# A decoder layer on one core: GpSimd takes the low half of the attention output and the first two normalisations, and the bias of v goes through the output weight once

## The reference, cut to what matters

```python
def attn(x, Wqkv, bqkv, Wo, bo):              # 16 heads of 32
    kqv = (x @ Wqkv + bqkv).reshape(b, s, 3, 16, 32)
    q, k, v = kqv[:, :, 0], kqv[:, :, 1], kqv[:, :, 2]
    scores = einsum('bsnh,btnh->bnst', k, q) / sqrt(32)
    scores = triu(scores) + -10000.0 * tril(ones, k=-1)
    attn = softmax(scores, axis=2)            # over s
    out = einsum('bnkq,bknh->bqnh', attn, v).reshape(b, s, 512)
    return out @ Wo + bo
def step(carry, kv_t):                        # wkv: a scan over t, per channel
    p, q, o = carry; kt, vt = kv_t
    no = maximum(o, u + kt); A = exp(o - no); E = exp(u + kt - no)
    y = (A * p + E * vt) / (A * q + E)
    no2 = maximum(w + o, kt); A2 = exp(w + o - no2); E2 = exp(kt - no2)
    return (A2 * p + E2 * vt, A2 * q + E2, no2), y
x = layernorm(x + attn(x))                    # x: 4 x 512 x 512, float32
x = layernorm(x + wkv(w, u, x, ctx))
x = layernorm(x + down(silu(gate(x)) * up(x)))  # inner width 2048
```

## Time and profile before

| | |
|---|---|
| median of 3 runs | 837.01 us (836.72 to 838.01) |
| the profiled execution | 835.81 us, its span 834.0 us |
| busy in the span | PE 743.1, DVE 558.8, ACT 408.3, POOL 271.2 us |
| granted TensorE clock, mean | 0.959 of full speed |

### The profile page before, as it was taken

How to read it: one execution, slowest core, us unless ns; L and a number is a source line. 1 busy time by engine, 2 the same in 40 slices (tenths; PEclk the granted TensorE clock), 3 DMA queues, 4 the chain that set the end, 5 groups by cost and what they waited for, 6 DMA issues and landing times.

```text
span 834.0 us, 11936 instructions
## 1 busy us (share of the span) xinstructions
PE 743.1 (89%) x4256; PEld 404.1 (48%) x4256; DVE 558.8 (67%) x1217; ACT 408.3 (49%) x1000; POOL 271.2 (33%) x284
## 2 busy tenths in 40 slices
PE   5988699978889978999677598889999999999997
PEld 2555456644456545565443254434454444444443
DVE  4455545778998879998898488874774544344434
ACT  5568767777567776686846213302332034104310
POOL 2001233328341155500346515541622133103320
PEclk9999799998999989999979899999999999999999
DMA  7246494232034122141620610001000100010001
GB/s 248 62 138 217 139 215 127 89 114 65 13 89 139 44 72 77 33 117 56 133 44 1 101 51 1 1 13 39 2 1 13 38 1 1 14 38 1 1 13 38
DMA packets 44331, 54.17 MB, mean 65 GB/s; under 512 B 4720, under 2 KB 33648, under 8 KB 44272
## 3 DMA queue, kind: packets, MB, share of 16 engines
q1 hardware_dynamic: 41008, 47.11, 18.0%
q0 software_dynamic: 3264, 6.29, 4.4%
HBM read 47.10 MB, written 12.58 MB: 72 GB/s over the span
## 4 chain that ended last, share of the span: by engine, by line
PE 59%; DVE 18%; issue 6%; POOL 6%; ACT 5%; DMA 3%; SPq 3%; POOLq 0%; DVEq 0%; ACTq 0%
PE psb L717 20%; PE psb L607 7%; PE psb L730 6%; PE psb L728 6%; PE psb L697 5%; PE psb L654 4%; DVE ek L1034 4%; DVE ee L946 3%; PE psb L621 2%; SPq L1270 2%; PE psb L643 2%; DMA xt<-in_xT 2%; PE psb L665 2%; PE psb L704 1%; PE psb L633 1%
## 5 line engine op out<-in xcount | busy, mean ns | idle before, releaser
L946 DVE CUSTOM_DVE_ANT_0 ee<-psb,mask,clip 128x512 f32<-128x512 f32 (+3 forms) x256 | 131.0, 530 | 54.7 <-PE psb L643 54.1
L810 ACT ACTIVATE ee<-ee,nm 128x512 f32<-128x512 f32 (+3 forms) x256 | 142.8, 559 | 32.4 <-DVE nm L946 32.1
L654 PE MATMUL psb<-ident,ee 128*128 128x128 f32 x640 | 108.5, 288 | 25.9 <-ACT ee L821 25.7
L821 ACT ACTIVATE ee<-psb 128x512 f32<-128x512 f32 (+1 forms) x192 | 100.0, 521 | 56.4 <-PE psb L654 56.1
L1212 POOL TENSOR_TENSOR hl<-hf,hh 128x512 f16<-128x512 f32 x64 | 77.5, 1211 | 134.9 <-ACT hh L884 134.9
L884 ACT ACTIVATE hh<-hf 128x512 bf16<-128x512 f32 x64 | 40.4, 632 | 144.1 <-DVE hf L1059 144.1
L717 PE MATMUL psb<-x2h,wg 128*128 128x512 f16 x256 | 99.5, 389 | 6.6 <-DVE th L1049 5.9
L654 PEld LDWEIGHTS psb<-ident,ee 128*128 128x128 f32 x640 | 76.3, 147 | 54.2 <-ACT ee L821 34.5
L717 PE MATMUL psb<-x2l,wg 128*128 128x512 f16 x256 | 99.7, 390 | 0.0
L730 PE MATMUL psb<-wd,hl 128*128 128x512 f16 x256 | 97.0, 379 | 2.3 <-POOL hl L1212 2.3
L717 PE MATMUL psb<-x2h,wu 128*128 128x512 f16 x256 | 97.5, 381 | 0.0
(11 more groups left out here) (106 smaller groups left out, 1236.3 us busy)
## 6 DMA issues: line engine op xcount, KB each, us to landing
qs<-parts SPq DMA_DIRECT2D x64, 128.0 KB, 2.7
ks<-parts SPq DMA_DIRECT2D x64, 128.0 KB, 2.9
parts<-qhl SPq DMA_DIRECT2D x16, 256.0 KB, 2.1
parts<-khl SPq DMA_DIRECT2D x16, 256.0 KB, 2.1
x<-in_x SPq DMA_DIRECT2D x4, 1024.0 KB, 7.8
ct<-in_ctxT SPq DMA_DIRECT2D x4, 1024.0 KB, 6.2
out<-x SPq DMA_DIRECT2D x16, 256.0 KB, 2.0
xt<-in_xT SPq DMA_DIRECT2D x14, 256.0 KB, 4.0
```

What stands on the lines that cost most here:

```text
L654: mm = e.transpose(PSB[:, bk, o:o + P], E[H % 3][:, EOFF[i] + j * P:EOFF[i] + (j + 1) * P], IDENT[:])
L810: e.activation(dst, dst, ACT.Exp, bias=NM[:, n % 4, col:col + 1], scale=-1.0, accum_out=DEN[:, n % 4, col:col + 1]).then_inc(sem("exp"), 1)
L821: e.activation(ET[h][:, base:base + width], PSB[:, bank["turn", H, item], 0:width], ACT.Copy).then_inc(sem("et"), 1)
L946: e.tensor_tensor_reduce(E[H % 3][:, EOFF[i]:EOFF[i] + w], PSB[:, bank["score", H, i], 0:w], MASK[:, S - w:S], -SC, CLIP[:, i:i + 1], ALU. ...
```

## The change

Four things are edited. `ol` becomes a plain subtraction on GpSimd, two slots after `normed` rather than four. `norm` of kinds 0 and 1 is done on GpSimd, directly behind `rstd`; kind 2 stays on VectorE. `oh` no longer adds the bias. Instead the bias is multiplied with the output weight once: four f32 matmuls (`bvo`) whose stationary operand is one column of `BV` repeated 128 times and whose moving operand is the f32 output weight in `CT`, and one add on VectorE (`bo`) into `BO`. `add_bo` waits for that add, and the load that overwrites `CT` waits for `bvo` as well.

```diff
     "pv": lambda n: ("t2", n),
+    "bvo": lambda: ("bo",),
...
         return lambda: (late(1, lambda: add("t3", n)), late(1 + hold, lambda: add("oh", n)),
-                        late(4 + hold, lambda: add("ol", n)))
+                        late(2 + hold, lambda: add("ol", n)))
...
                     if what == "split_wo":
-                        add("load_ct", 0)
+                        tt.unit("bvo")
+                        add("bvo")
+                        late(1, lambda: (add("bo"), add("load_ct", 0)))
...
+        def bvo():
+            emptied(("bvo",))
+            pe.wait_ge(sem("wo_in"), 16)
+            pe.wait_ge(*by_consts())
+            for k in range(T):
+                mm = e.matmul(PSB[:, bank["bvo",], :], BV[:, k:k + 1].broadcast_to([P, P]), CT[:, k, :], start=(k == 0),
+                              stop=(k == T - 1))
+            mm.then_inc(sem("bvo"), 1)
...
-            e.activation(oh[:, g, :], EB[:], ACT.Identity, bias=BV[:, g:g + 1]).then_inc(sem("oh"), 1)
+            e.activation(oh[:, g, :], EB[:], ACT.Copy).then_inc(sem("oh"), 1)
...
-        def o_low(n):
-            g = n % T
-            dve.wait_ge(*by("oh", n))
-            e.scalar_tensor_tensor(out=ol[:, g, :], in0=EB[:], scalar=BV[:, g:g + 1], in1=oh[:, g, :], op0=ALU.add,
-                                   op1=ALU.subtract).then_inc(sem("ol"), 1)
...
+            elif name == "bo":
+                dve.wait_ge(*by("bvo"))
+                dve.wait_ge(*by_consts2())
+                e.tensor_tensor(BO[:], PSB[:, bank["bvo",], :], BO[:], ALU.add).then_inc(sem("bo"), 1)
...
+        def norm(kind, b, t0, t1):
+            z = 4 * kind + b
+            pool.wait_ge(*by("rstd", kind, b, t0, t1))
+            for t in range(t0, t1):
+                e.tensor_scalar(X[b][:, t, :], X[b][:, t, :], MV[:, z, t, 0:1], RS[:, z, t:t + 1], ALU.subtract,
+                                ALU.mult).then_inc(sem(f"norm{kind}"), 1)
+
+        def o_low(n):
+            pool.wait_ge(*by("oh", n))
+            e.tensor_tensor(ol[:, n % T, :], EB[:], oh[:, n % T, :], ALU.subtract).then_inc(sem("ol"), 1)
...
-                pool.wait_ge(*by_consts2())
+                pool.wait_ge(*by("bo"))
...
                     sp.wait_ge(sem("wol"), T)
+                    sp.wait_ge(*by("bvo"))
```

More of the change, by code:

```diff
@@ L752, in _ @@
                 wo_part(*a)
+            elif name == "bvo":
+                bvo()
             elif name == "x1t":
@@ L1003, in rstd, with norm @@
             e.tensor_scalar(VE[:, z, t0:t1], MV[:, z, t0:t1, 1], EPS, None, ALU.add).then_inc(sem("ve"), 1)
-        def norm(kind, b, t0, t1):
-            z = 4 * kind + b
-            dve.wait_ge(*by("rstd", kind, b, t0, t1))
+        def norm(b, t0, t1):
+            dve.wait_ge(*by("rstd", 2, b, t0, t1))
             for t in range(t0, t1):
-                e.tensor_scalar(X[b][:, t, :], X[b][:, t, :], MV[:, z, t, 0:1], RS[:, z, t:t + 1], ALU.subtract,
-                                ALU.mult).then_inc(sem(f"norm{kind}"), 1)
+                e.tensor_scalar(X[b][:, t, :], X[b][:, t, :], MV[:, 8 + b, t, 0:1], RS[:, 8 + b, t:t + 1], ALU.subtract,
+                                ALU.mult).then_inc(sem("norm2"), 1)
         def scan_q(b, c):
@@ L1096, in _ @@
                 t3(*a)
-            elif name == "ol":
-                o_low(*a)
+            elif name == "bo":
+                dve.wait_ge(*by("bvo"))
+                dve.wait_ge(*by_consts2())
+                e.tensor_tensor(BO[:], PSB[:, bank["bvo",], :], BO[:], ALU.add).then_inc(sem("bo"), 1)
             elif name == "split_wo":
@@ L1116, in _ @@
                 rstd(*a)
-            elif name == "norm":
-                norm(*a)
+            elif name == "norm" and a[0] == 2:
+                norm(*a[1:])
             elif name == "scan_q":
@@ L1233, in _ @@
                 rstd(*a)
+            elif name == "norm" and a[0] != 2:
+                norm(*a)
+            elif name == "ol":
+                o_low(*a)
             elif name == "ek":
```

## The result

The change made the kernel slower: 860.66 us, median of four runs (857.04 to 861.06), against 836.87 us of the kernel before beside them (835.25 to 838.01). The ratio is 1.0276, with a 95% interval of 1.0244 to 1.0309: 23.8 us more, where 6 less were forecast. The profiled execution, the fastest of the four, took 857.04 us, its span 855.2 us.

A forecast was written before the change was run, and what follows sets the result against it. VectorE was taken to bound the attention's scan stretches, TensorE other parts, including everything from about 570 us. Terms -2.2 - 2.5 - 2.5 + 0.45 + 0.8 = -5.95 took 837.0 to 831.0 us; range 822 to 838.5.

The forecast's parts named there:

- The price of the norm: Norm instruction on GpSimd: 0.65 us each, four in 2.6 us against 1.92 on VectorE; upper bound 1.275 us.
- the rival at 840: Norms on GpSimd at the two-input price make the kernel slower: +2.9 us, 839.9 us; chance 0.12.
- The slower rival: Four norms on GpSimd take 5.1 us, making `d`, `x1t` and `hl` late: +2.9, 839.9 us; chance 0.12.
- Term A: Start of the feed-forward part: VectorE, freed of two norm holds, does its units earlier; -2.2 us, bounds 0 and -5.8.
- Term B: VectorE's full scan stretches without `ol`: -0.6 us for each of three scans, -0.7 before the third; -2.5 us.
- Term C: Five attention norms off VectorE: kind 1 -0.9 us each, kind 0 -0.2 to -0.3 each; -2.5 us together.
- Term D: What gets later: output product waiting for the last `ol`, +0.45 us; `ol` ahead of the last `xl`, +0.8.
- The bias through the weight: Four f32 products near 82 us cost nothing, as TensorE soon idles there; without that cover 4.2 us, once.

The follow-up runs named there:

- the run with the norms alone: The kernel before with only the norms of kinds 0 and 1 moved to GpSimd, as subtraction and multiplication; 855.67 us, 1.0219.
- the best version: The kernel before with only the norms of kinds 0 and 1 on GpSimd, written as addition then multiplication; 833.58 us, 0.9958.
- the run with the norms back: The changed kernel with all norms again on VectorE, `ol` on GpSimd and the bias through the output weight kept; 843.14 us, 1.0067.

## Why the prediction was wrong, point by point

- **The price of the norm is the step that failed.** I wrote that it "has one tensor input and two operations, as L1163 has", and so took 0.65 us, with 1.275 as the upper bound. It measured 2.11. The count of inputs and operations doesn't set the price; which operations they are does. L1163 multiplies and adds (0.65), the norm subtracts and multiplies. A bound "by the nearest two-input row" is no bound for another operation either: that was the worse fault, since it cut off the rival at 840.
- **The slower rival had the mechanism.** It named `d` behind the norm, three places, `x1t` and the second norm between two `hl`. With 8.3 us for four its own arithmetic gives 3 × 4.8 for `d` and 4.3 for `x1t`, 18.7 us; measured in the run with the norms alone: 4.8 at each of the three, 4.0, and 3.1 behind them, less 1.1 for each of the two norms of kind 1, where it had 0.9. Its point of decision, about 1.0 to 1.07 us an instruction, agrees with both sides measured in the kernel before: 0.82 us is faster, 2.1 slower. Nothing between was run.
- **Term A** (-2.2): by the price it became a loss of 4.0 us at the first norm. At 0.82 us the way from the first to the second inverse deviation took 5.6 us instead of 6.6, so 1.0 came back, and the 2.17 us wait of the earlier trace rows shrank to 1.41 and wasn't gone.
- **Term B** (-2.5) was wrong in itself for the order that the change has. Where -0.6 stood for each of three scans, the change measured -0.85, +0.8 and +0.7 (8.84 - 9.69, 8.51 - 7.73, 8.40 - 7.74). These three distances are the same within 0.02 us in the traces of all nine kernels with `ol` on GpSimd ahead of the denominator, and likewise in the five with it on VectorE. I put the denominator 1.3 us later, at 223.2, with the reciprocal free at 223.1. But beside VectorE's scans `ol` took 1.81 us, the product behind it 1.72 and the denominator 2.06, so that the reciprocal waited 0.85 us. The Trainium skill, "SBUF — State Buffer", section "Who interferes with whom", says that GpSimd and a two-input VectorE instruction exclude each other; by that rule I had worked out 0 for this term. The trace agrees with it as far as it goes (`ol` 1.16 us alone, 1.81 beside a scan), and the loss beyond 0 is the place in the queue: behind the denominator the same three distances are 2.5 us shorter than before (8.04, 7.29, 7.30). The whole kernel is no faster than before even so (1.0005); what takes the 2.5 us back isn't shown, and the bias through the weight is in that kernel too. The -0.7 for the `ol` ahead of the third scan wasn't measured apart.
- **Term C** (-2.5): the two norms of kind 1 gave 1.1 us each where -0.9 stood, at 0.82 us (milestones 265.85 to 282.47 before, 267.28 to 282.78 in the best version) and at 2.1 us as well (267.57 to 283.07 in the change). The three of kind 0 gave 0.4 each in the best version, where 0.2 to 0.3 stood, and cost 4.8 each at 2.1 us. That term was right, at its price. Terms A and C together stood at -4.7; the best version has -3.8.
- **Term D**: the wait of the output product for the last `ol` went from 3.8 to 4.2 us, +0.4, as forecast 0.45. The `ol` ahead of the last `xl` can't be read apart.
- **The bias through the weight** cost 0 to 3.4 us, 1.8 in the middle, where 0 stood; it is not settled whether it costs anything. The products themselves cost what I said or less (3.60 us for the four, at 80.15). If there is a cost, the traces point to the later load of `xt` in batch 3, of which the prediction says nothing.
- **Not in the sum at all**: the clock. After new waits TensorE can stand at its lower level for some microseconds, as behind the 4.40 us, and the mean granted clock of the change is 0.942 against 0.959. How much of the 24 us this is wasn't measured apart.

What stays open: how the 6 us of the run with the norms back divide. The place of `ol` ahead of the three denominators is 3.1 us against the place behind them, but only 0.6 against `ol` on VectorE. 1.7 are the stretch at the lower clock, with a cause that isn't shown. The rest is within what the bias may cost. I haven't run the cheap norm for kind 1 alone, or an `ol` in yet another place.

## What to carry to other kernels

A price taken from a row holds for its operations, not for its shape: before work is moved to another engine, put the exact instruction (operations, order, scalars) into a kernel and read its duration. On an in-order queue, ask of a moved block not who needs its result but what stands behind it; a block longer than the idle time ahead of the next urgent instruction only changes who waits when it is moved along. If a price is out of line, look for another way to write the same arithmetic: `(x - m) * r` as `(x + (-m)) * r` turned 2.1 us into 0.82. With the place of `ol` mended as well it turned a loss of 24 us into a small gain (0.9978), and alone in the kernel before it gave the best version (0.9958).

## What the runs showed of the hardware that I had not expected

- GpSimd's `tensor_scalar` on 128x512 f32, each as the median of its set: 0.62 us for add-multiply, multiply-add and multiply-multiply with constants (0.69 with one scalar from memory, 0.77 with two, 0.82 as the mean over a whole kernel); 1.48 to 1.49 for a single add, subtract or multiply; 1.91 to 1.93 for a pair with a subtraction, 2.07 to 2.08 with two scalars from memory. One operation costs more than twice what two out of add and multiply do. Single instructions beside the last scan took longer, 3.5 and 3.6 us with two scalars from memory. A subtraction by `tensor_tensor` with a repeated column took 1.07.
- The clock goes with the time of one and the same kernel: of the best version's twelve runs the nine with a mean granted clock of 0.952 to 0.959 took 832.3 to 834.5 us, the three with 0.946 to 0.948 took 836.0 to 837.0. It isn't all: the kernel before took 837.4 and 838.8 us in two runs at 0.960. The same idle time of TensorE was followed by the full clock in one kernel and by 0.83 in another. Differences of 1 to 2 us between kernels of this kind aren't told by single profiles.
